# Second attention: the multiply with the reciprocals of the sums on VectorE, with a new string of steps

## The reference, cut to what matters

```python
q = jnp.einsum('nhtc,hdc->nhtd', x, w_q)   # k and v alike; w_* are (16, 64, 128)
a = jnp.einsum('nhtd,nhsd->nhts', q, k) / jnp.sqrt(dk)
a = jnp.where(mask[None, None], -jnp.inf, a)
a = jax.nn.softmax(a, axis=-1)
y = jnp.einsum('nhts,nhsd->nthd', a, v)
y = y.reshape(y.shape[0], y.shape[1], -1)
return y @ w_o
```

## Time and profile before

| | |
|---|---|
| median of three runs | 766.88 us (765.96 to 769.78) |
| the profiled execution | 767.49 us, its span 765.70 us, granted clock 0.966 |
| TensorE (PE) busy | 696.4 us, 91% |
| VectorE (DVE) busy | 577.0 us, 75% |
| GpSimd (POOL) busy | 499.2 us, 65% |
| ScalarE (ACT) busy | 445.5 us, 58% |

### The profile page before, as it was taken

How to read it: one execution, slowest core, us unless ns; L and a number is a source line. 1 busy time by engine, 2 the same in 40 slices (tenths; PEclk the granted TensorE clock), 3 DMA queues, 4 the chain that set the end, 5 groups by cost and what they waited for, 6 DMA issues and landing times. The chain is left out here.

```text
span 765.7 us, 21921 instructions
## 1 busy us (share of the span) xinstructions
PE 696.4 (91%) x9509; PEld 413.8 (54%) x9511; DVE 577.0 (75%) x808; ACT 445.5 (58%) x536; POOL 499.2 (65%) x387
## 2 busy tenths in 40 slices
PE   2756888888889899999999999999999999999997
PEld 1523445444444454565655556556667555566774
DVE  7698897898998886778778777665676766774286
ACT  2333665988777769545655756555624565655511
POOL 6862245506854410389899999968981979999910
PEclk9856998999999999999999999999999999999999
DMA  8000000000000000001001011011101101101010
GB/s 275 8 1 2 3 2 3 2 3 3 2 3 3 2 3 3 3 3 30 3 30 30 3 29 32 4 29 30 31 3 30 30 3 30 30 6 45 12 29 29
DMA packets 13015, 15.68 MB, mean 20 GB/s; under 512 B 3000, under 2 KB 10488, under 8 KB 12920
## 3 DMA queue, kind: packets, MB, share of 16 engines
q1 hardware_dynamic: 12344, 13.96, 6.4%
q10 hardware_dynamic: 576, 0.33, 0.1%
HBM read 12.74 MB, written 1.16 MB: 18 GB/s over the span
## 5 line engine op out<-in xcount | busy, mean ns | idle before, releaser
L742 ACT ACTIVATE Pr<-ps 128x1024 f32<-128x1024 f32 (+1 forms) x258 | 237.8, 965 | 96.0 <-PE ps L1345 50.0
L1171 DVE TENSOR_REDUCE mxb<-ps 128x8 f32<-128x1024 f32 (+1 forms) x147 | 172.1, 1194 | 72.5 <-PE ps L1345 44.4
L725 POOL TENSOR_TENSOR V0s<-V0s,Pr 128x1024 f32<-128x1024 f32 x66 | 161.9, 2453 | 63.0 <-PE ps L1294 46.9
L1140 DVE TENSOR_REDUCE big<-ps 128x8 f32<-128x1024 f32 (+1 forms) x166 | 171.5, 1077 | 24.0 <-PE ps L1324 15.3
L1345 PE MATMUL ps<-big 64*128 64x128 f16 (+2 forms) x2560 | 169.0, 259 | 2.8 <-DVE mxb L1171 1.4
L1324 PE MATMUL ps<-big 32*128 32x128 f16 (+2 forms) x1280 | 102.0, 276 | 35.7 <-DVE big L1140 21.5
L1345 PEld LDWEIGHTS ps<-big 64*128 64x128 f16 x2560 | 92.1, 94 | 65.3 <-issue 22.1
L1324 PEld LDWEIGHTS ps<-big 32*128 32x128 f16 x1280 | 42.7, 95 | 108.6 <-ACT Pr L742 36.1
L1294 PE MATMUL ps<-Pr,V1s 128*64 128x256 f32 (+2 forms) x704 | 92.9, 404 | 0.4 <-ACT Pr L742 0.4
L725 POOL TENSOR_TENSOR acts<-acts,Pr 128x1024 f32<-128x1024 f32 x30 | 73.8, 2461 | 10.7 <-PE ps L1294 5.6
L1264 PE MATMUL ps<-Pr,V0s 128*18 128x128 f32 (+2 forms) x1280 | 80.3, 378 | 0.3 <-ACT Pr L749 0.3
(11 more groups left out here) (261 smaller groups left out, 1034.8 us busy)
## 6 DMA issues: line engine op xcount, KB each, us to landing
rec_b<-scratch_dram SPq DMA_DIRECT2D x28, 256.0 KB, 3.9
X<-in_x_dram SPq DMA_DIRECT2D x2, 256.0 KB, 3.5
big<-in_pick_rows_dram SPq DMA_DIRECT2D x2, 256.0 KB, 3.7
X<-in_x_dram SPq DMA_DIRECT2D x1, 512.0 KB, 6.3
rec_b<-in_w_q_dram SPq DMA_DIRECT2D x1, 512.0 KB, 6.1
XT<-in_w_k_dram SPq DMA_DIRECT2D x1, 512.0 KB, 6.9
XT<-in_w_v_dram SPq DMA_DIRECT2D x1, 512.0 KB, 8.0
wo_s<-in_w_o_dram SPq DMA_DIRECT2D x1, 512.0 KB, 9.2
```

The lines of the kernel that those rows point to most:

```text
L725: g.tensor_tensor(dst, dst, src, ALU.add).then_inc(summed, 1)
L742: ins = a.activation(dst[:, part], src, func, scale=scale)
L1140: ins = v.tensor_reduce(maxima_of(mall[:, r, 2 * u:2 * u + 2][:, part], i), block_view(src, i), AX.X, ALU.max, negate=True)
L1171: ins = v.tensor_reduce(maxima_of(mxb[:, r][:, part], arg), block_view(src, arg), AX.X, ALU.max, negate=True)
```

## The change

VectorE does the multiply of y_raw with rec_b that GpSimd did: norm_pair and its call leave GpSimd's program, and VectorE's loop gets the same instruction with the same two waits and the same semaphore, at the same step (exp chunk 1 of the pair two behind), ahead of the code for the low half. The string ORDER is replaced as a whole by another with the same letters in the same numbers.

```diff
@@ -214,17 +214,17 @@
 
 
 ORDER = (
-    "hhammmmmmhmmmmmmmmmamammmmmtememeeemhemmwmmwehemwemwmememwememewmeeheemwtmhmwhememwmheewemamewehmege"
-    "mwemwmemwmhmmmhmeemewehemtemmwemwhmhhhmhmememwhemewmegeemwhmhemewmhemwmeaeewmtememwmeememwemwmemwmee"
-    "emahewemwememewemewemmemwhemmtwwhemgemememwhemmwemgewmmhhamhheewehmewehmmewehemwmmhewememtwemememwme"
-    "amhemhhwemwemeeehmwememwmemwemwememheheewwmehtehhhhhhhwhhhwehmemgemhemwemeehwemwememewmemwemwememewm"
-    "mhhewmmQKQtVVMegeeMweMeweMeweMeweMeweMeweMeweeMgeewTKKQwwMMgEEEMWWMEEMWMMhMEEMEEMQKhTWhhWWWMEhMhhWWM"
-    "EMWSMEEEMWMEEMEEMMWWMMTWQhMWWMEMWWMEEMVhVhhVKWWWTSMEhEEMWMEEEEMWMMMWWWWMEEEEMQKhMWWWMEMWWSTMEMWMEEEh"
-    "hMWWWEhMKQhWWMEEMhEhVSTMEMWEEEEMWWWMMMWhWWMEhKQhhWWMhhEEMEhTSMEEhMWhWEMMWWMEEMWWWMEEEMVhWWEQKVSTEEMM"
-    "WWMEEEMWWMMMWWWMEEMEEESTQKWWWMMWWMEEEEMWMMMWWWMEEMEQVKVWWSTEMEEMWWMEEMEMWWWWWMEEEEEMWWMEEMQOKOSTMMWW"
-    "WEMMWWMMVQVKOOMMWWEMESThhEEMEEMEEEEMWWMMVhKQhWWWMMMWWWWEMEEEMSTMEEWWMEEEMKhWWWWMMMhWWWMEEMEhQVhhhWWT"
-    "SEMEEMWWMEEEMVhQhKhWhWWWWhMEEMWMMMWWEEMSTMEMWWMEEEEMWWWWMEEEMWWWWMEEMESTEEWWWWWEEVEEEEWWWWWXOXEEXFXh"
-    "FFEOFWWWWLXLLFXOFOLFFLFLLLL"
+    "hammmmmmmmmammmmmmammmmhmmthmememheehmemmewemmwmeewmewmemwmehmemeweemwmtemwmeheewmemheehwemwemaemgem"
+    "ewhemewemhmewmmhhmememweemwtmhmmwhhmhhmememwmememwehmehmwmeegmhewhmemamewemewtemewemewmememwmemwemem"
+    "heewemwemeemwmeaemmwmhmewwemetmhwmegememehmwmemwmegemhmhmamhheewhemwemwemmehewhmeewemmtehwemwmemweme"
+    "mamhmehwemehmweewhmehewemewemewemewemmmheetwemhhhhwhhhhhwhhehmemgmehemwmeehweemweemwemewhmemwemememw"
+    "mmhewmmQQKtVVMegeeMweMeweMeweMeweMeweMeweMeweeMgeewTQKKwwMMgEMEMWWMEEEEMWWMMhMEEMEMWMTQKhVhSMEhhMWhW"
+    "WWMEMhWMEEMEEMEEEMWMMMWWThQKVhWWMEMWhWWEEEMWhhWWMEEMSTMEMWWMEEEMWMMQhVKhhWWhWMEEMEEEMMWWTSMEEEEMWMMM"
+    "WWWhhVhWhWWMEEEMhQKhhhWWWMMWSTMEEEEhMWWWMEEMWMMQVKhWEMEhEMhMWWWTSMEEEMWWMEEEMWWWWMEEEEEVhMMWWQKVSTME"
+    "EMWWWMEEMMWWWWMMEWKQVWMEEMEEMSTMEMWMEEEMWWWWWWMEEEMWMEEMQKVTSMEEEEMWWWMMMWWWWWMEEEMWMEEMEKQVSTEMEMWW"
+    "WMMKQOOOOMMWMMWhWWWMEhEMEWWMEESTMEEMWWWMEEMQKhWWWMMEWEMEEMhhWWSTMEEEMhWWWMEEEMhhVhQVKMMWWWWMhEEMEEEM"
+    "MWWWWMESTMEMWWWMEEMWWMEEEEEMQKhWWSThWEMEEEhVVMMWWWhWWWMEEEEMWMMMWWWMESTEEEWhWWWWEEEEWWWWXEOXEEXEWFOF"
+    "FEhXLFWWWWXLLFXOFOLFFLFLLLL"
 )
 LEFT = {letter: iter(steps) for letter, steps in streams().items()}
 PLAN = [next(LEFT[letter]) for letter in ORDER]
@@ -558,11 +558,6 @@
                 steps[0] += 1
                 ins.then_inc(pool_step, 1)
                 pool.wait_ge(pool_step, steps[0])
-
-            def norm_pair(p):
-                pool.wait_ge(acc1_saved, p + 1)
-                pool.wait_ge(rec_in, 32 * (p + 1))
-                g.tensor_tensor(y_raw[p % 2], y_raw[p % 2], rec_b[:], ALU.mult).then_inc(normed, 1)
 
             def first_root(rows):
 
@@ -709,8 +704,6 @@
                     link(g.tensor_scalar(w_raw[key], w_raw[key], qk_scale[1][:, key:key + 1], None, ALU.mult))
                     g.tensor_tensor(w_parts[key][1], w_raw[key], w_parts[key][0], ALU.subtract).then_inc(w_split, 1)
                 if kind == "exp":
-                    if arg == NORM_AT and key >= 2:
-                        norm_pair(key - 2)
                     if arg < BASE or (key, arg) == (LAST, CH - 1):
                         continue
                     p, total = key, Psum[key % SETS]
@@ -1194,6 +1187,11 @@
                                            ALU.mult, ALU.add).then_inc(slot_dve, 1)
                     if k == WO_PARTS - 1:
                         dve.wait_ge(slot_dve, READS["V"][n])
+                if kind == "exp" and arg == NORM_AT and key >= 2:
+                    done = key - 2
+                    dve.wait_ge(acc1_saved, done + 1)
+                    dve.wait_ge(rec_in, 32 * (done + 1))
+                    v.tensor_tensor(y_raw[done % 2], y_raw[done % 2], rec_b[:], ALU.mult).then_inc(normed, 1)
                 if kind == "exp" and place_of(key, arg) == Y_LOW_AT[key == LAST] and key >= 2:
                     done = key - 2
                     dve.wait_ge(y_high, done + 1)
```

## The result

The changed kernel takes 777.6 us (776.0 to 780.1, four runs) against 766.9 us (766.0 to 769.8) for the kernel before: the ratio is 1.0136, with an interval of 1.0095 to 1.0176. That is 10.7 us more, and outside the predicted range of 757 to 774. The profiled execution took 780.1 us, with a span of 778.3 us and a granted clock of 0.950.

The account below looks back on a forecast made before the run. TensorE was taken as the bound, busy 396.32 of 400 us in the second attention. Terms -0.4 + 1.5 - 1.0 = +0.1 on the profiled 767.49, or 767.0 us on the median's scale; eight-in-ten range 757 to 774 us.

Parts of the forecast that it names:

- The string: Whole kernel: the new order has the same letters and work per engine; only two places can be read from the trace.
- the two places: First group's turn before its first exp, -1.0 us; and the end, where the last multiply's successors wait for TensorE, 0.
- The multiply's cost to TensorE, +1.5: Second attention: multiplies on VectorE delay score maxima; three at 0.51 us hold TensorE up, bounds 0 and 7.1 us.
- uncovered: A multiply with a single exp slot before the next row maximum, counted for pairs 3, 8 and 9.
- the second rival: Second attention: all fourteen multiplies, stretched beside GpSimd, cost TensorE 0.51 us each, 7.1 for 1.5: 772.6 us; chance 0.17.
- What leaves GpSimd, -0.4: Second attention: GpSimd loses fourteen multiplies, 34.1 us; TensorE gains only its own wait of 0.4 us, bounds 0 and 5.1.
- The multiply's own duration: VectorE's fourteen multiplies, taken at the mean of L1200, 2278 ns: 31.9 us in all, bounds 17.0 and 47.1.
- The wait for rec_b, 0: Before each multiply on VectorE: the slots since the reciprocal let rec_b land in time, so no cost; other end 4.5 us.
- The third rival: VectorE reaches the multiply before rec_b does and stands with the maxima behind it: +4.5 us, 771.5 us; chance 0.04.
- The first place, -1.0: First group's turn and exp: a score chunk between them saves VectorE's lost time, -1.0 us, bounds 0 and -2.9.
- The rest of the first attention, 0: First attention, 50 to 275 us, beyond its start: a reshuffle whose sign the trace does not give, taken as 0.
- the first rival: First attention: the new order feeds VectorE better, a third of the maxima's waits goes: -7.7 us, 759.3 us; chance 0.30.

Follow-up runs that it names:

- all three edits: Changed kernel, letters 568 to 575 and 682 to 692 reordered and the old string from letter 897 on: 776.8 us, ratio 1.0115.

## Why the prediction was wrong, step by step

**The string, the step that failed.** "It has the same 1027 letters with the same counts, so every engine has the same work; only the order changes, everywhere. Two places can be read." The sum then held the two places and an explicit 0 for the first attention, and no term for what another order costs in the second attention, from letter 470 on. With the multiply cut to 8 columns the new string costs 9.2 us, and 5.9 us of that is seen between the maxima of the two profiles (419.2 - 413.3); with the whole multiply it costs 5.1 us (777.6 - 772.5) on top of the old string's 5.3. The sign that would have shown it was named, TensorE at 395 us or more of 400, and it was 389.85. The prediction had the warning in its own first paragraph: 3.7 us of 400 were all that TensorE could be given back. Another order had almost nothing to win there and, as the run with the multiply on GpSimd shows, much to lose; equal counts say nothing of the waits. A rival on the slow side should have stood there, and none did. Why the new order is worse is shown only in part. It makes a dozen short waits for three engines, and taking some of them away didn't bring the time back; no single place explains the loss.

**The multiply's cost to TensorE, +1.5.** On the new string it is 777.6 - 776.2 = 1.4 us, with intervals that overlap, so it can't be told from 0. TensorE's waits for the maxima are 3.2 us, where "about 3" was forecast, but not at the places that were counted. The two longest:

```profile
382.03 0.40 PE L1343 MATMUL ps<-big 64*128 64x128 f16 x8 [0.93 <-DVE mxb L1164]
...
419.45 0.39 PE L1343 MATMUL ps<-big 64*128 64x512 f16 x2 [1.23 <-DVE mxb L1164]
```

The multiplies of pairs 3, 8 and 9 were to be uncovered. TensorE waits behind that of pair 9 (0.41 us), and not behind those of 3 and 8; the first line stands behind the one of pair 0, which three E were to cover and which took 3.38 us. The second line, and two waits of 0.31 and 0.33 us, stand behind no multiply, and are there with 8 columns too (1.24, 0.31 and 0.32 us). So 1.3 of the 3.2 us are the multiply's; that this is near the 1.5 is partly luck. On the old string the same multiply costs 5.3 us, 0.38 us each, where the second rival decides (0.37), and the waits for the maxima are 5.5. As the price of the move from engine to engine the term doesn't hold, for that depends on the order.

**What leaves GpSimd, -0.4.** No gain could be told (1.0001 with 8 columns on VectorE and nothing on GpSimd), within 0.15%. GpSimd's busy time fell by 24.2 us (20 to 30 forecast), ScalarE's wait at the rounding from 3.3 to 0.3 us. That fits the argument that TensorE had other work.

**The multiply's own duration.** 26.3 us against 31.9; the mean of 1877 ns lies just under the 1.9 to 2.6 us of the forecast, and the least and the most (1215, 3381) are those of the earlier trace rows. L1198 did not keep its mean: 2278 ns became 1902, and its median went from 2370 to 1280. GpSimd's lighter load did little of that: with the multiply on VectorE the median is still 1967 with the old string, and 1970 with the old one up to letter 470 and the new one behind it. So it hangs on what happens to run beside each instruction.

**The wait for rec_b, 0.** Counted in slots, the way looked long enough; measured, VectorE stood 10.8 us in four cases, over the 3 us that were to be the sign of an error. Of that, 6.1 us are at the last multiply, with no row maximum behind it, and 3.3 at pair 11, whose way the prediction had found the shortest. The size was wrong and the cost about right: 16.0 us of such waits went with an unchanged time. The third rival, +4.5 us for these waits, is not borne out. But they have a part in single waits of TensorE: in the 3.07 us with all three edits, and in 1.27 us on the old string, at 425.0 us, behind a multiply of 1.26 us that had waited 2.06 for rec_b.

**The first place, -1.0.** With a score chunk between the turn and its exp, TensorE's wait at the first exp shrank from 2.89 us to 1.53, and VectorE's from 0.97 to 0.30. In the timeline of the changed kernel:

```profile
63.97 0.61 PE L1322 MATMUL ps<-big 32*128 32x128 f16 x8 [1.53 <-issue]
...
65.47 1.23 DVE L1133 TENSOR_REDUCE big<-ps 128x8 f32<-128x1024 f32 x1 [0.30 <-PE ps L1322]
```

The step is right by itself (it was priced by VectorE's wait, which fell by 0.67 us), and lost again by the end of the stage (286.4 against 286.3 us on average).

**The rest of the first attention, 0, and the first rival.** The 0 holds on average. The rival asked for a third less of the maxima's waits for scores; they went from 23.1 us in 38 places to 24.8 in 40:

```profile
  PE ps L1322: 20.0, 33
  PE ps L1313: 4.8, 7
```

That the stage ended 4.6 us later in the profiled execution, over the 4 us that were named as a sign, was a scatter of that execution, as the ten others show.

## What to carry to other kernels

Where the engine that sets the pace is visibly idle for only 1% of a stage, price a new order of the steps on the slow side too, even when every engine keeps its work; moving work off an engine for which that one hardly waits need not gain anything. A string of steps belongs to the engines and durations that it is run with: change one part and keep the other before adding prices, since here the multiply on VectorE cost 5 us with the old string, the new string 9 with 8 columns of it and 33 with it on GpSimd, and the two together 11. And stalls that are mended one by one in a nearly full queue can move rather than vanish, so check the sum and not the place.

## What the runs showed of the hardware

The prediction said that the trace bears out only in part the rule of the Trainium skill, page "SBUF — State Buffer", section "Who interferes with whom", by which a VectorE instruction with two SBUF inputs and a GpSimd instruction that reads SBUF exclude each other, the later one waiting out the other. The 8-column multiply shows it plainly, since it needs 0.15 us by itself. VectorE and GpSimd in the timeline of the old string with 8 columns:

```profile
527.17 2.36 POOL L718 TENSOR_TENSOR V0s<-V0s,Pr 128x1024 f32<-128x1024 f32 x1 [0.17 <-POOL V0s L718]
```

```profile
527.48 2.07 DVE L1194 TENSOR_TENSOR Pr<-Pr,rec_b 128x8 f32<-128x8 f32 x1 [0.21 <-DMA rec_b<-scratch_dram]
```

The add ends at 527.17 + 2.36 = 529.53, the tiny multiply at 529.55: it was held to the add's end, and its wait is shown as duration. It goes the other way too. In the changed kernel a multiply is held by one add and holds the next:

```profile
373.94 3.13 POOL L718 TENSOR_TENSOR V0s<-V0s,Pr 128x1024 f32<-128x1024 f32 x1 [0.17 <-POOL V0s L718]
...
374.78 3.38 DVE L1194 TENSOR_TENSOR Pr<-Pr,rec_b 128x1024 f32<-128x1024 f32 x1
...
377.24 3.13 POOL L718 TENSOR_TENSOR V0s<-V0s,more_buf 128x1024 f32<-128x1024 f32 x1 [0.17 <-PE ps L1292]
```

The multiply ends at 378.16, some 1.1 us after the first add (377.07), about its lone time of 1.2; the next add takes 3.13 us where 2.36 is the lone time, 0.8 more. So a median between the ends need not be a partial stretch: here it mixes instructions that were alone with some that were held.

In the first attention of the changed kernel such a hold fell on the path: a VectorE instruction of 128x32, which takes 0.19 us elsewhere, lasted 2.07 beside a GpSimd multiply, and TensorE stood 2.02 us.

```profile
172.39 2.12 POOL L705 TENSOR_TENSOR wqkv<-rec_b,wqkv 128x1024 f16<-128x1024 f32 x1
172.49 2.07 DVE L1140 SCALAR_TENSOR_TENSOR big<-big 128x32 f16<-128x32 f32 x1
...
174.71 0.28 PE L1488 MATMUL ps<-idh_s,big 128*64 128x128 f16 x1 [2.02 <-DVE big L1140]
```

All eleven profiles with the new first letters have this hold. The six with the old ones have one near 120 us instead: in the kernel before the same instruction lasted 1.44 us at 119.73, and TensorE stood 1.72 us up to 122.52. From 174.4 to 180 us the granted clock of the changed kernel was 0.50, the lower level (1.2 GHz), and in the kernel before it was 0.50 from 123.6 to 130.4 us; in all 17 profiles it fell at the end of that stand of TensorE or soon behind it. So in the 25 us from 175 us on it was 0.67 after the change and 1.00 before, and the kernel before had its own fall elsewhere. That the hold made the clock fall is only argued: no run took it away and left the rest as it was.
